# Scores, maxima and exponentials handed over one head at a time, with the prologue, the pieces and the end chain in another order

## What is computed

```python
xq, xk, xv = (x @ w.T).reshape(B, T, 32, 16)      # q and k then rotary_pos_emb
scores = einsum('bqhd,bkhd->bhqk', xq, xk) * 16 ** -0.5   # causal mask, softmax over k
x = layernorm(x + einsum('bhqk,bkhd->bqhd', probs, xv).reshape(B, T, 512) @ wo.T)
xf = x / 128
inter = silu(xf @ w_gate.T) * (xf @ w_up.T)       # 1376 channels, ternary weights
inter_q = trunc(clip(inter * 128, -128, 127))
down = trunc(clip((inter_q @ w_down.T) * 128, -128, 127))
out = layernorm(x + down)
```

## Time and profile before

| | us |
|---|---|
| median of 3 runs | 416.82 |
| the profiled execution | 418.91 |
| its span, first to last instruction | 417.1 |
| PE busy | 374.8 (90%) |
| DVE busy | 255.9 (61%) |
| ACT busy | 217.6 (52%) |
| mean granted TensorE clock | 0.970 |

### The profile page before, as it was taken

The page is one execution under the profiler, slowest core; times in us unless marked ns, Lnnn a source line. Parts: engine busy times, 40 slices in busy tenths (PEclk is TensorE's granted clock), DMA queues, the critical chain, the costliest instruction groups (busy, mean ns, idle before and its releaser), DMA issues.

```text
span 417.1 us, 7212 instructions
## 1 busy us (share of the span) xinstructions
PE 374.8 (90%) x2532; PEld 289.0 (69%) x2532; DVE 255.9 (61%) x902; ACT 217.6 (52%) x355; POOL 83.5 (20%) x80
## 2 busy tenths in 40 slices
PE   7958866999999999978799988699999999999991
PEld 4746544777677776756577766488888888878880
DVE  5754865576667757694243526675555555548886
ACT  5866376766837677594344363345344444333331
POOL 3112012101303010352200100035233333111111
PEclk9989998999999999999899999599999999999997
DMA  8876758578570946949600040012222200000111
GB/s 279 294 118 136 145 84 138 65 155 113 79 132 13 164 97 119 198 52 229 137 2 8 6 152 1 2 50 77 77 75 72 65 32 8 24 2 27 67 60 50
DMA packets 79841, 37.60 MB, mean 90 GB/s; under 512 B 68672, under 2 KB 72896, under 8 KB 79808
## 3 DMA queue, kind: packets, MB, share of 16 engines
q1 hardware_dynamic: 76928, 35.08, 38.5%
q10 hardware_dynamic: 2880, 2.10, 2.5%
HBM read 17.24 MB, written 2.10 MB: 46 GB/s over the span
## 4 chain that ended last, share of the span: by engine, by line
PE 72%; DVE 8%; ACT 6%; DMA 5%; SPq 4%; issue 3%; POOL 1%; ACTq 0%; POOLq 0%; DVEq 0%
PE bank L832 8%; PE bank L834 6%; PE bank L833 6%; PE bank L968 5%; PE s_pair L832 4%; PE s_pair L833 4%; PE s_pair L834 4%; PE st_pair L833 4%; PE st_pair L832 4%; PE st_pair L834 4%; PE bank L1059 4%; PE bank L1060 4%; PE st_pair L949 3%; SPq L237 3%; DMA XR<-xT 3%
## 5 line engine op out<-in xcount | busy, mean ns | idle before, releaser
L631 DVE CUSTOM_DVE_ANT_0 SM<-s_pair,K 128x128 f32<-128x128 f32 (+1 forms) x256 | 76.2, 354 | 71.6 <-PE s_pair L935 71.6
L423 ACT ACTIVATE PTS<-st_pair 128x768 f32<-128x768 f32 x64 | 51.7, 809 | 44.0 <-PE st_pair L952 43.1
L319 POOL TENSOR_TENSOR RQ<-RQ,QS 128x256 f32<-128x256 f32 x32 | 21.9, 685 | 119.1 <-ACT QS L402 118.8
L545 ACT ACTIVATE f_a<-f_c 128x512 f32<-128x512 f32 x22 | 13.9, 632 | 59.6 <-DVE f_c L761 59.6
L832 PE MATMUL bank<-WQH,XH 128*128 128x512 f32 x88 | 38.6, 439 | 4.4 <-ACT V L394 4.4
L304 POOL TENSOR_TENSOR GL<-gu_raw,GH 128x1024 fp32r<-128x1024 f32 x11 | 26.6, 2417 | 78.2 <-ACT GH L466 78.2
L949 PE MATMUL st_pair<-identb,maskb 128*128 128x256 bf16 x128 | 35.8, 280 | 6.8 <-ACT PTS L423 6.6
L834 PE MATMUL bank<-WQH,XL 128*128 128x512 f32 x88 | 35.2, 400 | 0.0
L833 PE MATMUL bank<-WQL,XH 128*128 128x512 f32 x88 | 35.1, 399 | 0.0
L1059 PE MATMUL bank<-DH,IQ 128*128 128x512 f32 x88 | 34.4, 390 | 0.2 <-POOL DL L309 0.2
L1060 PE MATMUL bank<-DL,IQ 128*128 128x512 f32 x88 | 34.2, 389 | 0.0
(11 more groups left out here) (122 smaller groups left out, 880.8 us busy)
## 6 DMA issues: line engine op xcount, KB each, us to landing
gu_raw<-wgu SPq DMA_DIRECT2D x11, 512.0 KB, 4.5
w_raw<-wqkvo SPq DMA_DIRECT2D x6, 512.0 KB, 9.0
wd_raw<-wd SPq DMA_DIRECT2D x11, 256.0 KB, 3.2
RES<-x SPq DMA_DIRECT2D x4, 512.0 KB, 4.5
out<-o SPq DMA_DIRECT2D x8, 256.0 KB, 2.0
XR<-xT SPq DMA_DIRECT2D x3, 512.0 KB, 5.4
w_raw<-wqkvo ACTq DMA_DIRECT2D x4, 256.0 KB, 4.5
QT<-QS SPq DMA_TRANSPOSE x64, 3.7
```

What stands on the lines that cost most here:

```text
L423: nc.scalar.activation(PTS[:, u:u + 2, :], st_pair[:, :, 0:SW], ACT.Exp, scale=-1.0).then_inc(S["pr"], 1)
L631: last = nc.vector.tensor_tensor_reduce(out=SM[:, half, cols], in0=s_pair[:, half, cols], in1=above, scale=1.0, scalar=HUGE, op0=ALU.add, ...
```

## The change

- `exps` becomes two activations of 384 columns, one for each head; `sc`, `mx`, `stt` and `pr` count heads. `scores` and `shifted` wait for each half of a pair by itself. The scratch output `SM` becomes bf16.
- v of batch 1 goes to banks 2 and 3. `T1` has two buffers. The prologue's order on ACT and DVE is written out anew, with `x_hi(1)` ahead of `first_piece(0, 0, 1)`.
- The pieces run one item per step (steps 1 to 4 and 9 to 12) in place of one to two; third pieces in steps 3, 4, 5 and 11, 12, 13.
- In batch 3 gate and up start later, and only two of each remain in the steps; gate 2, up 2, gate 3 and up 3 run in parts between the steps of the end chain. `silu_up(2)` on DVE moves behind the residuals.

```diff
-DENSE = [...] + [("proj", 4 + t, 1, t, -1, 0) for t in range(NT)]
+DENSE = [...] + [("proj", 4 + t, 1, 2 + t, -1, 0) for t in range(NT)]
...
-        DENSE += [..., ("yt", 3, 0, 1, g + 4, 1)]
-        DENSE += [(kind, n, 0, int(kind == "up"), g + 5 + 3 * n + (kind == "up"), 2) for n in range(3) for kind in ("gate", "up")]
+        DENSE += [..., ("yt", 3, 0, 1, g + 5, 1)]
+        DENSE += [("gate", 0, 0, 0, g + 7, 2), ("up", 0, 0, 1, g + 9, 2), ("gate", 1, 0, 0, g + 11, 2), ("up", 1, 0, 1, g + 12, 2)]
...
-GU_STEPS = (3 * PAIRS - 1, 3 * PAIRS + 1, 3 * PAIRS + 5, 3 * PAIRS + 7)
-EARLY = 3
+GU_STEPS = (3 * PAIRS - 1, 3 * PAIRS + 1, 3 * PAIRS + 8, 3 * PAIRS + 12)
+EARLY = 2
...
 def sine(n, m, at):
-    wait(act, "rope", n * 4 + m)
+    wait(act, "rope", n * 4 + m - 1)
...
 def exps(p):
-    act.wait_ge(S["stt"], p + 1)
     wait(act, "pv", (2 * p - R_PTS) // 4 + 1)
-    nc.scalar.activation(PTS[:, u:u + 2, :], st_pair[:, :, 0:SW], ACT.Exp, scale=-1.0).then_inc(S["pr"], 1)
+    for half in range(2):
+        act.wait_ge(S["stt"], 2 * p + half + 1)
+        nc.scalar.activation(PTS[:, (2 * p + half) % R_PTS, :], st_pair[:, half, 0:SW], ACT.Exp, scale=-1.0).then_inc(S["pr"], 1)
...
+            sine(0, 0, DENSE[0][3])
+            w_hi(6)
+            first_piece(0, 0, 0)
+            sine(0, 1, DENSE[1][3])
+            w_hi(7)
+            x_hi(1)
+            first_piece(0, 0, 1)
+            second_piece(0, 0, 0)
+            sine(0, 2, DENSE[2][3])
+            sine(0, 3, DENSE[3][3])
+            second_piece(0, 0, 1)
+            first_piece(0, 0, 2)
+            first_piece(0, 0, 3)
+            second_piece(0, 0, 2)
             second_piece(0, 0, 3)
...
-                    for m in {1: [0], 2: [1, 2], 3: [3]}.get(s, []):
+                    for m in {1: [0], 2: [1], 3: [2], 4: [3]}.get(s, []):
                         first_piece(b, 1, m)
...
-                    for m in {3: [0, 1], 4: [2, 3]}.get(s, []):
+                    for m in {3: [0], 4: [1], 5: [2, 3]}.get(s, []):
                         third_piece(b, 1, m)
-                    for m in {11: [0, 1], 12: [2, 3]}.get(s, []):
+                    for m in {11: [0], 12: [1], 13: [2, 3]}.get(s, []):
                         third_piece(b + 1, 0, m)
...
 def scores(p):
-    wait(pe, "mx", p)
     for half in range(2):
+        wait(pe, "mx", 2 * p + half - 1)
...
-    last.then_inc(S["sc"], 1)
+        nc.tensor.matmul(to[:, P:SW], ...).then_inc(S["sc"], 1)
...
                 if g == NP + 2:
-                    gate(3, 3, 3, 0, 1)
-            pe.wait_ge(S["pr"], NP)
+                    gate(2, 2, 2, 0, 0)
+                if g == NP + LAG_ST:
+                    strips(bG[1], 3, 0, (0, 1))
+            strips(bG[1], 3, 0, (2, 3)).then_inc(S["g_mm"], 1)
             turn(TURN[-3])
+            pe.wait_ge(S["pr"], 2 * NP)
+            strips(bU[0], 2, 1, (0, 1))
+            turn(TURN[-2])
+            strips(bU[0], 2, 1, (2, 3)).then_inc(S["u_mm"], 1)
             turn(TURN[-1])
+            strips(bU[1], 3, 1, (0, 1))
+            for item in DENSE[-4:-2]:      # outp 0 and 1 of batch 3
+                for c in range(chunks(item)):
+                    dense(item, c)
+            strips(bU[1], 3, 1, (2, 3)).then_inc(S["u_mm"], 1)
+            for item in DENSE[-2:]:        # yt 6 and 7
+                dense(item, 0)
...
-            silu_up(2, 2, 2)
             truncate(0, 0, 0)
             residual(B - 1, 0, 0)
             residual(B - 1, 1, 1)
+            silu_up(2, 0, 2)
             for t in range(NT):
                 layernorm(B - 1, t)
```

More of the change, by code:

```diff
@@ L64 @@
 R_PTS = 8
-DENSE = [("proj", m, 0, (0, 1, 4, 5, 0, 1)[m], -1, 0) for m in range(6)] + [("proj", 4 + t, 1, t, -1, 0) for t in range(NT)]
+DENSE = [("proj", m, 0, (0, 1, 4, 5, 0, 1)[m], -1, 0) for m in range(6)] + [("proj", 4 + t, 1, 2 + t, -1, 0) for t in range(NT)]
 TURN = []
@@ L232, in stacks @@
                 b, o = divmod(k, OCTS)
-                wait(sp, "stt", 4 * (k - OCTS) + 4)
+                wait(sp, "stt", OCT * (k - OCTS) + OCT)
                 for a in range(2):
@@ L330, in _ @@
                 if b < B:
-                    for m in {1: [0], 2: [1, 2], 3: [3]}.get(s, []):
+                    for m in {1: [0], 2: [1], 3: [2], 4: [3]}.get(s, []):
                         rest(b, 1, m)
                 if b + 1 < B:
-                    for m in {9: [0, 1], 10: [2], 11: [3]}.get(s, []):
+                    for m in {9: [0], 10: [1], 11: [2], 12: [3]}.get(s, []):
                         rest(b + 1, 0, m)
-                if b + 2 < B and s == 13:
+                if b + 2 < B and s == 14:
                     x_lo(b + 2)
@@ L385, in sine @@
                 act.wait_ge(S["proj"], n * 4 + m + 1)
-                wait(act, "rope", n * 4 + m)
+                wait(act, "rope", n * 4 + m - 1)
                 sin = K[:, K_ROT + 4 * t + 2 * a + 1:K_ROT + 4 * t + 2 * a + 2]
-                nc.scalar.activation(T1[:, :], bank[at][:, :], ACT.Copy, scale=sin).then_inc(S["t1"], 1)
+                nc.scalar.activation(T1[:, m % 2, :], bank[at][:, :], ACT.Copy, scale=sin).then_inc(S["t1"], 1)
             def values(n, t, at):
@@ L512, in _ @@
                             second_piece(b, 1, m - 1)
-                    if s == 3:
+                    if s == 4:
                         second_piece(b, 1, 3)
                 if b + 1 < B:
-                    for m in {9: [0, 1], 10: [2], 11: [3]}.get(s, []):
+                    for m in {9: [0], 10: [1], 11: [2], 12: [3]}.get(s, []):
                         first_piece(b + 1, 0, m)
@@ L519, in _ @@
                             second_piece(b + 1, 0, m - 1)
-                    if s == 11:
+                    if s == 12:
                         second_piece(b + 1, 0, 3)
-                if b + 2 < B and s == 12:
+                if b + 2 < B and s == 13:
                     x_hi(b + 2)
@@ L551, in _ @@
             chan_hi(B - 1, 1)
-            silu(2, 2)
             magnitude_and_sign(0)
+            silu(2, 0)
             silu(3, 1)
@@ L628, in maximum @@
                 for half in range(2):
+                    dve.wait_ge(S["sc"], 2 * p + half + 1)
                     for t, cols in ((0, slice(0, P)), (1, slice(P, SW))):
@@ L712, in _ @@
             dve.wait_ge(S["k_in"], 16)
[L713 to L723, removed]
+            rotate(0, 0, DENSE[0][3])
+            w_lo(6)
+            rotate(0, 1, DENSE[1][3])
+            w_lo(7)
+            dve.wait_ge(S["xh"], 1)
+            nc.vector.tensor_tensor(XL[1][:, :, :], XR[1][:, :, :], XH[1][:, :, :].bitcast(F32), ALU.subtract).then_inc(S["xl1"], 1)
+            third_piece(0, 0, 0)
+            rotate(0, 2, DENSE[2][3])
+            rotate(0, 3, DENSE[3][3])
+            for m in range(1, 4):
+                third_piece(0, 0, m)
             w_lo(8)
@@ L856, in weights_by_y, with strips @@
                 return product(dst[:, :], c, wh[:, k, c, :], wl[:, k, c, :], YH[half][:, c, :], YL[half][:, c, :])
+            def strips(dst, slot, k, which):
+                for c in which:
+                    last = weights_by_y(dst, slot, k, c, 0)
+                return last
             def dense(item, c):
@@ L934, in scores @@
                     nc.tensor.matmul(to[:, 0:P], q[:, 0:P], k[:, 0:P], start=True, stop=True)
-                    last = nc.tensor.matmul(to[:, P:SW], q[:, P:T], k[:, 0:T], start=True, stop=True)
-                last.then_inc(S["sc"], 1)
+                    nc.tensor.matmul(to[:, P:SW], q[:, P:T], k[:, 0:T], start=True, stop=True).then_inc(S["sc"], 1)
             def shifted(p):
@@ L943, in shifted @@
                     pe.wait_ge(S[f"mq{g % 2}"], 16 * (g // 2 + 1))
-                wait(pe, "pr", p)
                 for half in range(2):
+                    wait(pe, "pr", 2 * p + half - 1)
                     q = QT[g % OCTS][0:MROWS, 0, (2 * j + half) % OCT, :]
@@ L951, in shifted @@
                     nc.tensor.matmul(to[:, 0:P], k[:, 0:P], q[:, 0:P], start=False, stop=True)
-                    last = nc.tensor.matmul(to[:, T:SW], k[:, 0:P], q[:, P:T], start=True, stop=True)
-                last.then_inc(S["stt"], 1)
+                    nc.tensor.matmul(to[:, T:SW], k[:, 0:P], q[:, P:T], start=True, stop=True).then_inc(S["stt"], 1)
             def pv(q):
```

29 lines of the change are left out of this document (12 added, 17 removed).

## The result

The changed kernel takes 404.47 us, median of 4 runs (402.9 to 408.38), against 417.19 for the kernel before in the same session. The ratio is 0.971, with a 95% interval of 0.963 to 0.980. The forecast was 403.8, in a range of 397 to 412. The profiled execution took 403.42 us, with a span of 401.6.

The account below looks back on a forecast made before the run. PE bounds batch 2; gains can come only from prologue, batch 0, batch 3 and end chain. Terms -4.3 + 0 - 10.2 + 1.5 = -13.0 give 405.9 profiled, 403.8 us as median; range 397 to 412.

Parts of the forecast that it names:

- Prologue: Start to `scores(0)`: PE's 4.38 us gap goes, the transposing DMA is late next; `scores(0)` at 29.65, 4.8 us earlier.
- ACT's new wait: Prologue: ACT, there at about 16.5, waits for the data of `x_hi(1)`, landing at 18.25; 1.75 us.
- Batch 0: `scores(0)` to step 16: last DMA only 3.9 us earlier, 0.4 gained by exponentials; 4.3 us earlier at step 16.
- The hand-over by head: Batch 0's ACT-bound steps: dearer split exponential costs some 1 us, earlier starts give back rather more; 0.4 us gained.
- Batches 1 and 2: PE-bound stages: added hand-overs free and later third pieces just fit; 0 change, ends -1 and +4 us.
- without that cover: `x_hi`, `x_lo` one step later: free behind 6 us of PE work before the next projection; otherwise 1.1 on ACT per batch.
- The rival of stacks late at seven places: `scores` waits for the DMA at steps 8, 16, 24, 32, 40, 48, 56, 1 us each; +6, 410; chance 0.16.
- Batch 3: Gate 2 and up 2 leave, waits for YL and ACT shrink, `scores(56)` waits; -10.2 us, ends -13 and -6.
- ACT's wait at up 0: Batch 3: ACT's 3.91 us wait for the last transposing DMA goes, up 0 being evacuated in step 58; -3.8 us.
- The new wait before `scores(56)`: Batch 3: third piece, two DMAs and landing take 8.5 to 9 us against about 7 of PE work; +1.5 us.
- End chain: End of attention: 5.5 us of moved matmuls return, 3.8 into gaps, 0.3 for `silu_up(2)`; +2.0, with low clock +1.5.
- The low clock at the start of the feed forward: Behind the end chain, at 266.58, costing 2.7 us before: expected again, perhaps shorter; -0.5 us.

Follow-up runs that it names:

- e4: The kernel before with only the change's batch 3 and end chain (gate and up later, split steps, silu_up 2); 409.49 us, ratio 0.985.
- e1: The kernel before with the hand-over by head alone (two exponentials of 384 columns, counts by head, SM in bf16); 414.24 us, ratio 0.994.
- e7: The kernel before with only the banks of v of batch 1 changed, 2 and 3 for 0 and 1; 416.02 us, ratio 1.000.
- the repeat: The changed kernel once more, unchanged, on the chip of three of the variants; 404.76 us, ratio 0.972.
- e2: The changed kernel with the hand-over by pair as before, one exponential activation and SM in float32; 409.65 us, ratio 0.984.
- e3: The kernel before with the change's prologue alone: banks 2 and 3, two T1 buffers, new ACT and DVE order; 412.23 us, ratio 0.993.
- e10: The changed kernel with old first-half piece steps, x_hi and x_lo in steps 14 and 15, 16 spare matmuls around step 0; 405.19 us, ratio 0.974.
- e6: The changed kernel with x_hi in step 14 and x_lo in step 15; 405.4 us, ratio 0.976.
- e8: The changed kernel with the first half's pieces and x_hi in their old steps, the second half's one per step; 402.15 us, ratio 0.971.
- e11: As e10, with 44 more spare matmuls in steps 10 to 15 of batch 0; 404.04 us, ratio 0.972.

## Why the prediction was right

**Prologue: right in each step.** PE through at 28.4 (28.2 and one matmul), ACT's new wait 1.75 (1.80), `scores(0)` at 29.65 (29.67). The match to 0.02 is luck: the kernels with the new prologue and no spare matmuls start at 29.67 to 30.42, those with the old one at 34.45, 35.24 (e4) and 35.34 (e1). I did not price the low clock behind the remaining gap, which in e7 cost 2.6 us in two steps and made nothing of the banks.

**Batch 0: right place, size open.** I had ACT released by the batch's last DMA 3.9 us earlier than the 57.14 of the earlier trace rows; it was 4.1 (53.08), and 3.1 in the repeat (54.02). The batch is 1.9 us shorter in the first profile and 1.0 in the repeat, against a forecast of 0.5 longer. One price was wrong: two activations of 384 columns were put at 0.98 us together and take 0.87, 0.06 more than one of 768 and not 0.17. The hand-over by head, priced at 0.4, gives 0.6 in step 9 alone, which is shown; in the whole batch it gives 1.3 us (e2's 37.92 against 36.61) or 0.4 (against the repeat's 37.50). The rest can't be told from single profiles: e4, whose batch 0 is that of the kernel before, has 36.88 us in place of 38.52, and the hand-over by head alone (e1) 35.81.

**Batches 1 and 2: wrong by 2.9 us (2.1 in the repeat), inside the bound of 4.** I asked of the later third pieces only whether `scores` would wait for their DMAs. At steps 24, 32, 40 and 48 it did not, but ACT did, 0.88 us in step 26, ahead of `QS`, and that is a part of step 30. What I had put at nothing, `x_hi` one step later, cost 0.9, and the first half's pieces moved into steps 28 and 44 cost 0.8 and 0.9. I had argued from PE's work ahead of the next projection, and named 1.1 us of ACT "without that cover"; the cover that was missing was another one, step 29 with no dense work, and `chan_hi` queued behind `x_hi`. The rival of stacks late at seven places is refuted at its price: only `scores(56)` waited, 0.22 us, and in the repeat `scores` 8, 16 and 56, 0.52, 0.42 and 0.16, where it had 1 us at each of seven.

**Batch 3: right, with one term too many.** Forecast -10.2, measured -11.1, and -9.2 with this part alone. ACT's wait at up 0 is down from 3.91 us to 1.38 and ends with a DMA that lands just behind PE's last matmul of up 0; PE is busy throughout steps 58 and 59, so it costs nothing, and the low clock of 204 us is gone:

```profile
199.06 0.60 ACT L461 ACTIVATE f_v<-bank 128x512 f32<-128x512 f32 x1 [1.38 <-DMA QT<-QS]
```

The new wait before `scores(56)`, put at 1.5 us, was 0.22: steps 53 to 55 lasted 8.7 us and not the 7 that I had counted, and its path of 8.5 to 9 fits into that. The kernel before was a little unlucky in its profile here: in e1, e3 and e7, which leave this part alone, ACT waited 2.2 to 3.0 us at up 0 and not 3.91, and the stretch took 55.4 to 56.2 us, so of the 11.1 some 2 are of that one execution.

**End chain: right sign, 1.2 us less.** The hand-over by head gave 0.6 of it: the chain is 39.55 us with and 40.19 without it. Without it, that is 1.5 longer than before, so the gaps took little more of the moved matmuls than the 3.8 of 5.5 that I had counted (Y from 2.53 to 1.8, OL and OT to nothing). The low clock at the start of the feed forward lasted from 252.3 to 255.7 us, where it had lasted from 262.3 to 272.5; the feed forward is 1.4 us shorter. I had -0.5, and much of either may be chance: with the new end chain this part took 150.5 us (e4) to 147.6 (e10), with no low clock in e6, e8, e10 and e11, and with the old one 150.5 (before) and 149.4 (e1, e7).

**The sum** was right partly because errors cancelled: batches 1 and 2 lost 2.9 us that I had put at 0, and batch 0 (2.4), batch 3 (0.9), the end chain (1.2) and the feed forward (0.9) each came out shorter than forecast. The difference of medians is 12.7 us, the forecast 13.0; the two profiled executions differ by 15.5.

## What to carry to other kernels

On an engine that runs its queue in order, a step is only as hidden as the work of the others in that same step: before moving work by a step, look at how long the step it moves into is for the engine that bounds the kernel, and at what stands behind it in its own queue. When a transfer comes later, ask not only who reads what it writes but also who may overwrite what it reads. When a wait is removed, work out what is late next and how much the bounding engine does until then; behind a gap and thin work the low clock fell in e7, and took back everything. Handing over halves of a tile paid where two engines alternate (step 9, the end chain) and cost nothing where one is saturated.

## What the runs showed of the hardware

- Two activations of 384 columns right behind each other take 0.87 us, not twice the 0.49 that one takes; one of 768 takes 0.81. The fixed part mostly overlaps.
- On a saturated PE 22 more increments and 22 more waits, all satisfied, cost nothing: 33.81 us and 33.81; with 32 more in batch 2, 49.71 and 49.71 (e1).
- Whether the low clock falls into a thin stretch differs between executions of one kernel, by 1.3 us in one step (2.14 and 3.42).
